# Cross-attention and a routed feed-forward layer on one core: another order of the steps in which attention ends and the expert slots begin

## The reference, cut to what matters

```python
def reference(x, ctx, Wq, bq, Wk, bk, Wv, bv, Wd, bd, w_red, wg, W1, b1, W2, b2):
    x = x + xattn(layernorm(x), ctx, ctx, Wq, ..., bd)
    return x + ffn(layernorm(x), w_red, wg, W1, b1, W2, b2)

def xattn(q, k, v, ...):            # x, ctx: 32 tiles of 128 tokens, 256 channels, f32
    query, key, value = q @ Wq.T + bq, k @ Wk.T + bk, v @ Wv.T + bv
    # 16 heads of 16; for each token the 16 heads of the query meet the 16 heads of the key
    logits = einsum('bsid,bsjd->bsij', query, key) / sqrt(16)
    out = einsum('bsij,bsjd->bsid', softmax(logits), value)
    return transpose(out).reshape(B, -1, 256) @ Wd.T + bd

def ffn(h, ...):                    # 8 experts, hidden size 512, one expert for each token
    gates = softmax((h @ w_red) @ normalized(wg).T)
    scores, idx = max(gates), argmax(gates)
    o = gelu(h @ W1[idx] + b1[idx]) @ W2[idx] + b2[idx]
    return o * scores
```

## Time and profile before

| | us |
|---|---|
| median of three runs | 436.13 (432.74 to 436.34) |
| the profiled execution: its own time | 435.58 |
| the profiled execution: span from first to last instruction | 433.7 |
| PE busy | 384.0 (89%) |
| DVE busy | 312.9 (72%) |
| POOL busy | 297.8 (69%) |
| ACT busy | 234.6 (54%) |

### The profile page before, as it was taken

The page is one execution under the profiler, slowest core; times in us unless marked ns, Lnnn a source line. Parts: engine busy times, 40 slices in busy tenths (PEclk is TensorE's granted clock), DMA queues, the critical chain, the costliest instruction groups (busy, mean ns, idle before and its releaser), DMA issues.

```text
span 433.7 us, 11372 instructions
## 1 busy us (share of the span) xinstructions
PE 384.0 (89%) x3785; PEld 306.2 (71%) x3785; DVE 312.9 (72%) x667; ACT 234.6 (54%) x781; POOL 297.8 (69%) x399
## 2 busy tenths in 40 slices
PE   3998799999999889899797587988999999999990
PEld 3776577666767667656565475777999999999970
DVE  0564899988989889999999774578465555556640
ACT  2334378868768587777562465563244444444420
POOL 1568668869779587786765965565377777777751
PEclk9699899999999999999999898999899999999996
DMA  5776668697796788966575500131012222222200
GB/s 168 228 201 200 159 186 225 204 243 197 211 242 193 203 210 229 249 187 166 160 169 164 149 27 26 50 115 50 26 63 76 74 69 66 68 66 68 66 18 0
DMA packets 97513, 59.31 MB, mean 137 GB/s; under 512 B 70446, under 2 KB 88527, under 8 KB 97456
## 3 DMA queue, kind: packets, MB, share of 16 engines
q1 hardware_dynamic: 92336, 48.44, 40.9%
q0 software_dynamic: 3744, 9.53, 7.5%
q10 hardware_dynamic: 1376, 0.61, 0.5%
HBM read 37.41 MB, written 22.07 MB: 137 GB/s over the span
## 4 chain that ended last, share of the span: by engine, by line
PE 46%; DVE 16%; DMA 14%; issue 10%; POOL 7%; SPq 3%; ACT 2%; DVEq 1%; ACTq 0%; POOLq 0%
PE bQ L1079 14%; DMA qkv_scr<-qkv 10%; PE bKV L1047 8%; PE bL L1047 6%; PE bKV L897 4%; POOL kx L368 4%; DMA ql<-qkv_scr 2%; PE bL L905 2%; DVE qkv L472 2%; PE bO L905 2%; PE bY L933 2%; PE bQ L969 2%; DMA wgT<-in_L_ffn_wg 2%; SPq L244 2%; PE bT L1061 2%
## 5 line engine op out<-in xcount | busy, mean ns | idle before, releaser
L368 POOL TENSOR_TENSOR kx<-ql,mask 128x2048 f32<-128x2048 f32 x32 | 117.9, 3683 | 40.0 <-issue 28.3
L1079 PE MATMUL bQ<-w,wA 128*128 x312 | 74.3, 381 | 3.3 <-DVE r L712 2.7
L462 DVE TENSOR_TENSOR ax<-bA,mask 128x2048 f32<-128x2048 f32 x32 | 73.3, 2290 | 0.6 <-PE bA L985 0.6
L1079 PEld LDWEIGHTS bQ<-w,wA 128*128 128x128 f32 x312 | 56.2, 190 | 10.6 <-issue 4.5
L897 PE MATMUL bKV<-wA,xcT 128*128 128x512 f32 x128 | 61.9, 607 | 1.4 <-DVE qkv L472 1.4
L391 POOL DMA_INDIRECT out<-r,isc x39 | 41.3, 1059 | 22.3 <-issue 13.4
L349 POOL TENSOR_TENSOR rs<-ve,half 128x2 f32<-128x2 f32 x39 | 28.3, 726 | 24.9 <-ACT ve L733 24.8
L414 POOL DMA_INDIRECT r<-row_scr,ig x39 | 40.5, 1038 | 6.0 <-issue 2.4
L842 ACT ACTIVATE wA<-bL,r 128x128 f32<-128x128 f32 x76 | 21.6, 367 | 41.3 <-PE bL L1047 26.6
L842 ACT ACTIVATE wA<-bKV,r 128x128 f32<-128x128 f32 x80 | 22.8, 368 | 37.6 <-PE bKV L1047 20.8
L905 PE MATMUL bO<-ax,pad 128*32 128x128 f32 x1024 | 36.2, 284 | 6.7 <-DVE ax L462 6.4
(11 more groups left out here) (200 smaller groups left out, 726.9 us busy)
## 6 DMA issues: line engine op xcount, KB each, us to landing
qkv_scr<-qkv SPq DMA_DIRECT2D x32, 384.0 KB, 3.5
ql<-qkv_scr SPq DMA_DIRECT2D x32, 384.0 KB, 4.4
row_scr<-cat SPq DMA_DIRECT2D x32, 133.5 KB, 3.5
w<-in_L_ffn_W SPq DMA_DIRECT2D x16, 256.0 KB, 4.5
xt<-in_x SPq DMA_DIRECT2D x15, 256.0 KB, 4.8
ct<-in_ctx SPq DMA_DIRECT2D x15, 256.0 KB, 5.4
w1b<-in_L_ffn_W SPq DMA_DIRECT2D x12, 256.0 KB, 4.3
w1b<-in_L_ffn_W SPq DMA_DIRECT2D x2, 512.0 KB, 7.8
```

What stands on the lines that cost most here:

```text
L368: eng.tensor_tensor(block(kx[:, z % 2, :]), spread_heads(ql[z % 2][:, :, 0:HD]), mask_b, ALU.mult).then_inc(S["kx"], 1)
L462: eng.tensor_tensor(block(ax[:, :]), spread_heads(bA[:, 0:C].rearrange("p (l i) -> p l i", l=NH)), mask_b, ALU.mult).then_inc(S["ax"], 1)
L1079: i_ = eng.matmul(bQ[:, 0:C], hT[b % 2][:, k, :], w2[:, bass.ds(eb * (KH * C) + k * C, C)], start=(k == 0), stop=(k == KH - 1))
```

## The change

Five lists are reordered; nothing is computed differently.

1. POOL: the first gather moves from the end of step 31 to step 32, behind the power and its copy and before the spreading of the keys. The second gather goes with the third, at the end of step 32.
2. ACT: from step 32 on the finishing of a row (`scalar_row`, L772 to L782) comes after the placing and the exponential of the step, not before them.
3. PE: within the steps up to 38 the rows of slot n are turned one step later, right behind the next logits, in the same step as up n. One call after the last step keeps the count.
4. DVE: gT is taken out of `vector_up` and becomes `vector_turned`; within the steps it stands behind the subtraction of the maximum, one step later than before, ahead of the residual. In the plain loop it directly follows w1s as before.
5. DVE: at the end of a step yo comes first and w1s second. In the plain loop the order of w1s, gT and yo stays.

```diff
@@ pool_attention
+                if t == FIRST + 1:
+                    pool_gather(eng, 0)
@@ pool_ffn
-            for a in (0, 1) if s == 0 else (s + 1,):
+            for a in () if s == 0 else (1, 2) if s == 1 else (s + 1,):
@@ vector_attention
                     eng.tensor_tensor(lg, lg, mx[:, :].unsqueeze(2).broadcast_to((P, NH, NH)),
                                       ALU.subtract).then_inc(S["lsub"], 1)
+                for s in SLOTS_AT.get(t, ()):
+                    vector_turned(eng, s - 2)
                 if live(w):
...
                 for s in SLOTS_AT.get(t, ()):
+                    vector_down(eng, s)
                     vector_up(eng, s)
-                    vector_down(eng, s)
+            vector_turned(eng, LAST - FIRST - 1)
@@ vector_up
                 eng.tensor_scalar(w1s[n % 2], w1f[:, bass.ds(ex * W1W, W1W)], 1.0, None,
                                   ALU.mult).then_inc(S["w1s"], 1)
+
+        def vector_turned(eng, n):
+            if slotted(n):
                 eng.wait_ge(S["gtr"], n + 1)
@@ scalar_attention
-                if live(d):
-                    eng.wait_ge(S["rs"], t + 2)
-                    r = rs[t % 3][:, 1:2]
...
+                if live(d) and t < NT:
+                    scalar_row(eng, t, d)
...
                     eng.activation(pr, bL[:, 0:C], ACT.Exp, scale=HD ** -0.5).then_inc(S["exp"], 1)
+                if live(d) and t >= NT:
+                    scalar_row(eng, t, d)
+
+        def scalar_row(eng, t, d):
+            eng.wait_ge(S["rs"], t + 2)
+            r = rs[t % 3][:, 1:2]
...
@@ tensor_attention
                     blocks(eng, bL, pad[:, s0 % 3, 0:2 * C], kx[:, s0 % 2, :]).then_inc(S["qk"], 1)
+                slots = SLOTS_AT.get(t, ())
+                for s in slots:
+                    tensor_rows(eng, s - 1)
...
-                slots = SLOTS_AT.get(t, ())
                 for s in slots:
                     tensor_up(eng, s)
                     tensor_down(eng, s)
-                for s in slots:
-                    tensor_rows(eng, s)
...
+            tensor_rows(eng, LAST - FIRST)
@@ the plain loop of DVE
                 vector_up(eng, s)
+                vector_turned(eng, s - 1)
```

More of the change, by code:

```diff
@@ L823, in scalar_attention @@
                 eng.wait_ge(S["score"], d + 1)
+        def scalar_row(eng, t, d):
+            eng.wait_ge(S["rs"], t + 2)
+            r = rs[t % 3][:, 1:2]
+            eng.wait_ge(S["nm1"], d + 1)
+            eng.activation(cat[d % CR][:, NB_:NB_ + 1], nm[:, 1:2], ACT.Copy, scale=r).then_inc(S["nb"], 1)
+            eng.wait_ge(S["gsub"], d + 1)
+            if d < HOLD:
+                eng.activation(ge[:, :], glog[:, d, :], ACT.Exp, scale=r,
+                               accum_out=cat[d % CR][:, SC:SC + 1]).then_inc(S["score"], 1)
+            else:
+                eng.activation(gsc[:, d - HOLD, :], glog[:, d, :], ACT.Copy, scale=r).then_inc(S["scaled"], 1)
         def scalar_rows(eng, s):
```

## The result

Over 20 runs of each kernel on the same chips the median is 441.5 us after the change and 436.23 before. The ratio of the two is 1.0108, with a 95% interval of 1.0082 to 1.0134, so the change costs 3.6 to 5.8 us. Two of the 20 runs after (444.19 and 447.8) fell in a slower state of the chip and are left out of that ratio. The profiled execution after has a span of 439.7, before 433.7.

The account below looks back on a forecast made before the run. PE bounds the even part, DVE from gT 7 on, so gT 7's time decides. Down 1 gains 0.95, then the closed PE-DVE loop makes up 6 later by 4.3: 436.13 + 4.3 = 440.4, range 436.0 to 443.5.

Parts of the forecast that it names:

- Keys 31: POOL's spreading of the keys of tile 31 was to start at 247.7 instead of 248.26.
- the bounds I gave: Gain from POOL's reordered gather: at best 0.98 (keys 31 at 247.3), at the other end nothing (248.26).
- the held gather: On POOL, w1s 0 would now meet POOL's product and hold the gather behind it, so keys 31 start at 247.7.
- Down 0: On PE, behind w1s 1, DVE's expansion and Gelu 0: from 258.96 to 258.35, 0.6 earlier.
- Down 1: On PE, after the last value product and up 2: 269.80 less 0.95, so 268.85.
- DVE's first wait: After down 0, DVE does yo 0, w1s 2, then the last expansion, which starts at 262.28, 0.9 earlier.
- PE's 4.10 wait: PE's wait ahead of the first turned rows, in step 32; was to shrink to about 1.7, but off the path.
- The loop: PE and DVE wait in turn: down n-2 to up n 4.50, ups 6.28 apart, up 6 later by 4.3.
- The clock: Rival, 22%: PE's clock falls in the new waits of slots 4 and 6; one fall gives 442.0, two 443.5.
- The old times kept: Rival, 16%: ACT sets the slot distances of 4.7 to 5.7, the loop doesn't close; only 0.95 counts, 435.2.
- the even pace: Rival, 8%: three slot distances shrink to 3.73, gaining 4.1, with the 0.95 that is 5.0: 431.1.

Follow-up runs that it names:

- the kernel with the spare products: Changed kernel plus an unread 512-column product on DVE behind w1s 3, 4 and 5; stage (first routing index to up 9) 77.08, against 75.26 in the changed kernel.

## Why the prediction was right

- **The time.** 440.4 was forecast, 441.5 measured, inside the range. A difference of 4.3 was forecast, and 3.6 to 5.8 is measured.
- **What earns.** Keys 31 earlier by 0.56 was forecast, by 1.0 measured: the end of the bounds I gave, since the product on POOL no longer meets w1s (0.75 instead of 1.2), which made up for the held gather. Down 0 was to gain 0.6 and gained 0.99. Down 1 was to be at 268.85, the old index assumed; with the index 0.99 later it is 269.75 - 0.99 = 268.76. That it fits to 0.1 is partly luck: the last expansion started 1.26 earlier against the index and not 0.91 (the prediction writes 0.9 and then subtracts 0.95), and up 2 took 2.79 and not 2.56, at a granted clock of 0.70. The price for DVE's first wait (w1s 2 between yo 0 and the expansion) was right.
- **Whose gain it is.** I put the end of PE's 4.10 wait down to part 2 and said that it isn't the path, and I put the gain of down 0 down to part 1. The run with parts 1 and 2 alone shows that they leave 2.90 of the wait, and that 0.10 of a gain reaches down 0; the new places of rows and gT are needed. The sum didn't suffer, since all parts were in.
- **The loop.** 4.50 from down to up was forecast, 4.42 to 4.44 measured in slots 3, 4 and 6. Distances of 6.28 against 6.30, 6.65 and 6.28. The middle one was mis-sized by 0.35: between yo 3 and w1s 5 DVE idled 0.63 at "issue" instead of 0.27. The same place shows 0.62 in the kernel with the spare products, so it isn't chance, but I have no cause for it. Up 6 came 4.5 later than before against the index (4.3 forecast), the stage 4.6.
- **Part 5 as the cause.** The sum put the whole loss on DVE's order at the end of a step. With that order alone the stage is 76.54, and with everything but that order 68.66.
- **The rivals.** The clock: PE idled 2.33, 1.78 and 2.31 and each of the next ups took 2.02 at a granted clock of 1.00, so it did not happen in the traced execution. The range has about 1.6 for one fall (442.0 against 440.4) and twice that for two; no trace shows such a fall in the new waits, and what was measured is 1.3 to 1.6 for one that comes between the last value product and down 1. The old times kept, and the even pace: the ups are 6.3 to 6.7 apart, so neither; and the swap alone, which leaves ACT's list as it was, has the same distances.
- **What I missed.** There was 3.6 to be had at down 1, and not 0.95, had w1s stayed ahead of yo: 30.10 against 33.69. Part 5 cost 2.5 there already: w1s 2 stood between yo 0 and the last expansion, which put the last value product 0.95 later (28.16 against 27.21 from the index), and behind that longer idle time (2.86 against 1.89) PE's granted clock was 0.62 until down 1, against 1.00, and that stretch took another 1.6.

## What to carry to other kernels

An engine's list is a queue: an operation put behind one that waits for another engine inherits that wait, as w1s 4 did the 2.86 of yo 2 for down 2. Before swapping two operations, write down who needs each and whose end each waits for; if B's user is the engine that A waits for, A ahead of B ties the two engines into a loop whose length is the sum of both (6.28 added up, 6.28 to 6.65 measured). Work without that wait (the weight copy here) goes in front of it, where it was free here, and the cheapest test is a spare operation in either place. Here it added 0.6 to a distance in the one and nothing in the other (stage 68.62 against 68.66).

## What the runs showed of the hardware

**The clock isn't told by the last idle time alone.** At the last value product PE idled 2.86 to 2.97 in five traces, and the clock fell in all five: within the product in three (it took 1.90 or 1.94 instead of 1.08), and later in two (product 1.23 and 1.08, then up 2 took 3.50 and 3.40 instead of 2.05). The granted clock from the product to down 1 was 0.62 to 0.67 in these five. Behind an idle time of 1.89 to 2.02 it stayed at 1.00 in six traces. But in the kernel with w1s 1 behind the expansion, after the same 1.89, it fell one instruction group later. Windows of that trace (us, busy PE, granted clock, DMA):

```profile
262.00:264.00 2.00, 2.00 (x15) 0.61 0.18 66
264.00:266.00 2.00, 2.00 (x10) 0.54 0.00 0
```

Up 2 and down 1 stand there, and down 1 came 3.21 behind up 2 instead of 1.88: that is the 1.3 that this kernel's stage is longer. And longer idle times cost nothing elsewhere: behind 2.33 and 2.31 in the changed kernel, and behind 2.93 ahead of up 4 in the changed kernel with the spare products, the granted clock of the up was 1.00. On the latter's timeline of PE both sorts stand:

```profile
262.50 1.08 PE L920 MATMUL bO<-ax,pad 128*32 128x128 f32 x32 [2.86 <-DVE ax L465]
263.51 3.40 PE L1063 MATMUL bKV<-wA,r 128*128 128x128 f32 x16
...
278.97 2.02 PE L1063 MATMUL bKV<-wA,r 128*128 128x128 f32 x16 [2.93 <-DVE wA L712]
```

It even falls without an idle time: behind the long row of L1029 matmuls, which stand back to back, up 9 took 2.99 to 3.66 in eleven traces (granted clock 0.50 in 306.77 to 308.50 of the trace before) and 1.97 in one, that of part 5 alone. So the price of an idle time near 2 can't be told in advance here; where the clock fell at the last value product, the way to down 1 took 4.2 to 4.5 instead of 2.9, so 1.3 to 1.6 more.

**The weight copy and POOL held each other up.** Called 1.27 after keys 31 began, w1s 1 lasted 2.95; called 2.70 after, 1.52; in both it ended 0.56 behind their end. It went the other way round too: in the kernel after, POOL's copy of one column took 0.66 instead of 0.18 when w1s 0 was ahead of it, and ended at 244.24, 0.04 behind w1s 0 (243.33, 0.87 long).
